# Four attention layers over eight images on one core: a fourth place for the exponentials, and a later plan for the side work

## The reference, cut to what is computed

```python
x = layer0(x)   # group norm, qkv, 8 heads of 32 channels, projection, + x
x = layer1(x)   # below
x = layer2(x)   # group norm, qkv, 8 heads of 32 channels, projection, + the normed x
x = layer3(x)   # group norm, qkv, ONE head of 256 channels, projection, + x

def layer1(h):
    x = group_norm(h) + pos_emb
    s = sigmoid(conv1x1(silu(conv3x3(silu(conv1x1(x))))))      # spatial weights
    sh = group_norm(x)
    standard = attention(sh @ wq, sh @ wk, sh @ wv)            # 8 heads of 32
    multi = [attention((x * s) @ wq_i, sh @ wk_i, sh @ wv_i) for i in (0, 1)]   # 2 heads of 128
    fused = silu(concat(standard, multi) @ ff_w1 + b1) @ ff_w2 + b2
    return group_norm(fused @ out_w + out_b) + h
```

## Time and profile before

| what | us |
|---|---|
| median of 3 runs | 5251.7 |
| lowest and highest run | 5237.88, 5256.1 |
| the profiled execution, its own time | 5264.05 |
| span of its trace, first to last instruction | 5262.3 |
| PE busy in the span | 4914.8 |
| mean granted clock of PE, as a share of full | 0.948 |

### The profile page before, as it was taken

One profiled execution on the slowest core, in us unless ns is written; L12 is line 12 of the kernel. 1 busy time (PEld: TensorE's weight loads), 2 busy tenths in 40 slices (PEclk: granted clock), 3 DMA queues, 4 the chain that ended last, 5 costly groups with the idle time before them and its releaser, 6 DMA issues. The chain is left out here.

```text
span 5262.3 us, 62946 instructions
## 1 busy us (share of the span) xinstructions
PE 4914.8 (93%) x22016; PEld 2254.5 (43%) x22016; DVE 3047.0 (58%) x5432; ACT 2418.6 (46%) x4321; POOL 2868.2 (55%) x1649
## 2 busy tenths in 40 slices
PE   7789999999999999999999999999999999999888
PEld 3325334553335533354334633346333463345424
DVE  6455666366773666636665467555666456763462
ACT  3352555435553455524555245552555425553251
POOL 3472567436664466634667357563666535764362
PEclk8899989999999998999999999899989999999988
DMA  3111212021210211102210112201122012110110
GB/s 88 27 35 46 55 37 55 16 60 45 51 37 21 75 42 40 37 26 64 55 43 20 41 49 57 49 13 47 49 51 55 7 53 57 46 46 11 30 36 12
DMA packets 103606, 221.18 MB, mean 42 GB/s; under 512 B 31104, under 2 KB 33408, under 8 KB 103168
## 3 DMA queue, kind: packets, MB, share of 16 engines
q1 hardware_dynamic: 103296, 217.16, 16.0%
HBM read 56.47 MB, written 8.39 MB: 12 GB/s over the span
## 5 line engine op out<-in xcount | busy, mean ns | idle before, releaser
L855 ACT ACTIVATE probs<-bank 128x512 f32<-128x512 f32 x3456 | 1934.5, 599 | 2401.5 <-PE bank L517 2279.4
L958 DVE TENSOR_REDUCE max_cols<-bank 128x1 f32<-128x512 f32 x3456 | 2191.5, 681 | 1367.4 <-PE bank L517 1360.0
L1200 POOL TENSOR_TENSOR probs_added<-probs_added,probs 128x1024 f32<-128x1024 f32 x768 | 1796.8, 2373 | 83.5 <-ACT probs L855 83.4
L517 PE MATMUL bank<-q_stack,k_stack 97*128 97x512 f32 (+1 forms) x3584 | 1674.2, 523 | 63.8 <-DVE max_cols L958 32.1
L517 PE MATMUL bank<-probs,v_tokens 128*32 128x512 f32 (+1 forms) x7168 | 1373.7, 639 | 31.5 <-ACT probs L855 29.9
L1200 POOL TENSOR_TENSOR probs_added<-probs 128x1024 f32<-128x1024 f32 x192 | 454.0, 2370 | 1042.0 <-ACT probs L855 1040.3
L517 PEld LDWEIGHTS bank<-q_stack,k_stack 97*128 97x128 f32 (+1 forms) x3584 | 665.2, 195 | 799.7 <-issue 442.6
L517 PE MATMUL bank<-act,weight_stream 128*128 128x512 f32 x1792 | 937.1, 625 | 38.6 <-ACT act L865 27.4
L1187 POOL TENSOR_TENSOR probs_added<-probs_added,probs 128x512 f32<-128x512 f32 x288 | 368.4, 1279 | 623.5 <-ACT probs L855 622.2
L517 PE MATMUL bank<-high_parts 32*128 32x512 f32 x3072 | 403.7, 513 | 120.1 <-DVE max_cols L958 82.0
L517 PEld LDWEIGHTS bank<-probs,v_tokens 128*32 128x32 f32 (+1 forms) x7168 | 317.0, 122 | 444.4 <-issue 306.2
(11 more groups left out here) (84 smaller groups left out, 2929.9 us busy)
## 6 DMA issues: line engine op xcount, KB each, us to landing
k_stack<-high_parts SPq DMA_DIRECT2D x384, 128.0 KB, 2.4
q_stack<-high_parts SPq DMA_DIRECT2D x768, 64.0 KB, 2.0
weight_stream<-stream_dram SPq DMA_DIRECT2D x32, 768.0 KB, 4.3
k_stack<-low_parts SPq DMA_DIRECT2D x192, 128.0 KB, 2.4
q_stack<-low_parts SPq DMA_DIRECT2D x384, 64.0 KB, 2.0
act<-x_dram SPq DMA_DIRECT2D x8, 1024.0 KB, 6.5
act<-pos_dram SPq DMA_DIRECT2D x8, 1024.0 KB, 5.8
weight_stream<-stream_dram SPq DMA_DIRECT2D x16, 512.0 KB, 3.9
```

The source lines that it names most:

```text
L517: return nc.tensor.matmul(dst, lhsT, rhs, start=start, stop=stop, **kw)
L855: act.activation(PR[:, m % P_RING, j, :], bank[:, :], ACT.Exp, scale=att.scale).then_inc(reading(key), 1)
L958: dve.tensor_reduce(cols[:, kh, j, qt:qt + 1], bank[:, :], AX.X, ALU.max).then_inc(reading(key), 1)
L1200: pool.tensor_tensor(ADD[:, js, :], one, two, ALU.add).then_inc(p_added, 1)
```

## The change

PR gets a fourth place. Its memory is that of WLO, so SBUF use stays as it was. Narrow attentions use all four places, wide ones the first three; `places_of_probs` picks for each item the place that was used longest ago, and notes the item that was there before (`PRIOR`), for which ACT waits. DVE gets one wait, before it writes the first low part of k of "m": until PE and POOL are done with the last item in the fourth place. In the plan of between-work "1" the convolutions spread out, the second norm comes later, and q, k, v start 3 units later; in that of "2", q, k, v start 1.8 units later and the first quads 1 unit earlier. No instruction is added or removed on any engine but for these waits, and none changes its size.

```diff
-P_RING = 3
+P_RING = 4
...
-            each("stats", [("a",) + q for q in QUARTERS], 42, 1) + unit("sa1", 0, 2, 44) + unit("sa1", 1, 2, 46.5) + \
-            norm("norm", 47.2, 2.5, "a", "o") + unit("sa2", 0, 3, 54.5) + unit("sa2", 1, 3, 57.5) + \
-            tile("sa3", 0, 1, 63.6) + tile("sa3", 1, 1, 66.1) + [(65.9, "sa3 one", 0), (68.4, "sa3 one", 1)] + \
-            each("spatial", QUARTERS, 68.8, 1)
-        out = [(at + (4.8 if name == "apply" and i[0] == "norm" else 0), name, i) for at, name, i in out]
-        out += projections(group(0), 71.1, 1) + stacks(80, 2.3) + values(82.1, 2) + projections(group(1), 109.1, 1.7) + \
+            each("stats", [("a",) + q for q in QUARTERS], 41.5, 1.5) + unit("sa1", 0, 2, 43.5) + unit("sa1", 1, 2, 47.5) + \
+            norm("norm", 50.2, 2.5, "a", "o") + unit("sa2", 0, 3, 56) + unit("sa2", 1, 3, 59.5) + \
+            tile("sa3", 0, 1, 65.6) + tile("sa3", 1, 1, 69.1) + [(67.9, "sa3 one", 0), (71.4, "sa3 one", 1)] + \
+            each("spatial", QUARTERS, 71.8, 1)
+        out = [(at + (3.2 if name == "apply" and i[0] == "norm" else 0), name, i) for at, name, i in out]
+        out += projections(group(0), 74.1, 1) + stacks(82.5, 2.1) + values(84.1, 2) + projections(group(1), 109.1, 1.7) + \
             narrow_start(87, 120.5, 118, 4)
...
-            projections(group(0), 76.8, 1) + stacks(85.5, 2) + values(87, 2) + projections(group(1), 110.1, 1.6) + \
-            narrow_start(88, 121.5, 118, 4)
+            projections(group(0), 78.6, 1) + stacks(87, 1.8) + values(88.6, 1.9) + projections(group(1), 110.1, 1.6) + \
+            narrow_start(87, 121.5, 118, 4)
...
+def places_of_probs():
+    place, prior, last = [], [], [None] * P_RING
+    for m, (att, _) in enumerate(ITEMS):
+        p = min(range(P_RING - att.wide), key=lambda p: -1 if last[p] is None else last[p])
+        place.append(p)
+        prior.append(last[p])
+        last[p] = m
+    return place, prior
...
-        WLO = sb("wide_low", [P, CT, T], F32R)
...
+        WLO = sb("wide_low", [P, CT, T], F32R, at=pr_at + (P_RING - 1) * 4 * HALF * 4)
...
-                if j == 0 and m >= P_RING:
-                    act.wait_ge(p_used, m - P_RING + 1)
-                    added = added_before(*ITEMS[m - P_RING])
+                if j == 0 and PRIOR[m] is not None:
+                    act.wait_ge(p_used, PRIOR[m] + 1)
+                    added = added_before(*ITEMS[PRIOR[m]])
...
+                    if att.kind == "m" and name == "k" and i == (0, 0):
+                        m = max(m for m in range(att.item0) if PLACE[m] == P_RING - 1)
+                        dve.wait_ge(p_used, m + 1)
+                        dve.wait_ge(p_added, added_before(*ITEMS[m]))
```

More of the change, by code:

```diff
@@ L252 @@
 ITEMS = [(a, i) for a in ATTS for i in range(a.units // 4)]
+def places_of_probs():
[6 more added lines that the diff above has]
+    return place, prior
+PLACE, PRIOR = places_of_probs()
 def plan():
@@ L576, in narrow_probs @@
             def narrow_probs(att, s, i):
-                return PR[:, (att.item0 + 8 * s + i) % P_RING, :, :]
+                return PR[:, PLACE[att.item0 + 8 * s + i], :, :]
             def values_narrow(att, s, i):
@@ L606, in values_wide @@
                 keys = [("av", att.index, s), ("av2", att.index, s)][:att.ctiles]
-                probs = PR[:, (att.item0 + 2 * s + kt // 4) % P_RING, kt % 4, :]
+                probs = PR[:, PLACE[att.item0 + 2 * s + kt // 4], kt % 4, :]
                 for d, key in enumerate(keys):
@@ L854, in score @@
                 bank = until_full(act, key)
-                act.activation(PR[:, m % P_RING, j, :], bank[:, :], ACT.Exp, scale=att.scale).then_inc(reading(key), 1)
+                act.activation(PR[:, PLACE[m], j, :], bank[:, :], ACT.Exp, scale=att.scale).then_inc(reading(key), 1)
             for event, it, i in PLAN:
@@ L1180, in score @@
                     until_read(pool, key)
-                    one, two = (PR[:, (att.item0 + v // 4) % P_RING, v % 4, :] for v in (u - 1, u))
+                    one, two = (PR[:, PLACE[att.item0 + v // 4], v % 4, :] for v in (u - 1, u))
                     if r == 1:
@@ L1193, in score @@
                     m, js = att.item0 + u // 4, slice(j - 1, j + 1)
-                    one, two = PR[:, (m - 1) % P_RING, js, :], PR[:, m % P_RING, js, :]
+                    one, two = PR[:, PLACE[m - 1], js, :], PR[:, PLACE[m], js, :]
                     if i == 1 and j == 1:
```

## The result

The changed kernel takes 5192.2 us (median of 4 runs, 5188.1 to 5196.6) beside 5244.8 for the kernel before on the same chip: a ratio of 0.9892, 95% interval 0.9867 to 0.9916, or 52.6 us less. The forecast was 5150. The time lies outside the forecast's own range (5120 to 5185) and inside the range for 8 in 10 (5092 to 5218), 42 us from the forecast and 10 from the rival "the clock falls as before" (5202).

A forecast was written before the change was run, and what follows sets the result against it. PE's idle time (347.5 us) and half clock (274 us) were taken as the bound. Savings of 56 + 29 + 23 = 108 us gave 5156, and half of 12.35 more gave 5150; own range 5120 to 5185, 8 in 10 5092 to 5218.

The forecast's parts named there:

- the clock falls as before: Rival, chance 0.25: idle time goes (55 us), but half clock lasts as long as before; some 5202 us.
- The sum: Whole kernel: 56 (between-work "1"), 29 (between-work "2") and 23 us (fourth place) make 108 us saved.
- What bounds the kernel: Whole kernel: PE's idle time, 347.5 us, and half clock, 274 us; attention "1" beside "3" at full clock.
- Idle time at unit 50: Between-work "1", units 49 to 53: PE's waits fall from 3.43 to 1.2 us, saving 15 us over seven stretches.
- The clock behind it: After unit 50's waits, attention "2" beside "1": four of seven clock falls go, 41 of 71.6 us.
- The argument from attention "1": Attention "1" beside "3": similar idle time, spread over a stretch, goes with clock 1.00; used to support the 41 us.
- q, k, v of between-work "2": Attention "0" beside "2": the 3.00 us before k's first product falls to 0.6, 17 us, plus 12 of clock: 29.
- The fall at unit 40 ... I keep: Attention "0" beside "2": the half-clock stretch at unit 40, 13.7 us in the row shown, stays.
- The fourth place, alone on the engines: Three attentions running alone: some 7.8 us less each, 23 us in all; waits move from ACT to PE.
- In the loaded stretches ... I count 0: Attentions beside between-work: the fourth place gives 0, as POOL is far from busy there.
- The jam at unit 66: Rival, chance 0.08, units 64 to 68: a new PE stop and clock fall cost 19 us a sample; 5342 at full price.
- What would show it.: Signs: attention "2" about 156.5 us at clock 0.95 or more in most, "0" near 159, attentions alone about 8 less each.

The follow-up runs named there:

- group 2: Runs on one chip: kernel before (mean 5255.0 us), the changed kernel again (5206.5), and three variants of the changed kernel (5203.9, 5205.9, 5159.0).
- the repeat: The changed kernel measured again without further edits, six runs beside the kernel before: mean 5206.5 us, ratio 0.9906 (0.9887 to 0.9926).
- the later statistics: Changed kernel with the residual's statistics 2 units later, norm and q, k, v 1 unit later in between-work "2": 5205.9 us, 0.9905 of before.
- the lighter steps: In attentions running alone POOL makes eight adds, not ten; PE multiplies the item by ones: 0.9811 of before on the changed kernel, 1.0037 on the kernel before.
- split mixes: Changed kernel with the three DVE instructions of each sa1 mix in three successive units: mean 5203.9 us, 0.9902 of before.
- group 3: Runs on one chip: kernel before (25 runs, mean 5239.7 us) and four kernels with edits to POOL's adds (5163.9, 5223.9, 5189.4, 5258.7).

## Why the prediction was right, and where it was wrong

- **The sum.** The 108 us were 55 of idle time and 53 of clock (41 and 12). In the means of group 2 the change takes 49 us: 38 at full clock and 11 of clock. Both terms were too large, the second most. That 5150 came within 42 us owes something to luck: the first four runs lost only 225 us to half clock, six later ones 242.
- **What bounds the kernel.** Right in the main: idle time of PE and its clock. "3" beside "m" stayed as it was. Attention "1" beside "3", untouched by the edit, didn't: one of seven stretches had 6.8 us of half clock, and in the repeat's profile three of seven, up to 13.6 us.
- **Idle time at unit 50.** 3.43 us went to 1.96 (1.22 + 0.49 + 0.25), where I put 1.2. The quad's wait was to fall to 0.3 and rose from 1.02 to 1.22: at unit 47 the mix comes right behind the last statistics of the convolution's input, which I left out of DVE's account, and "mean" now waits for its own "aggr". "var" lost its 1.68 as foreseen.
- **The clock behind it.** This is the step that failed: "I take four of seven falls as gone", 41 us. None went. 143.1 us at half clock became 112.8 at that place, and another 34.0 appeared near unit 67 behind 0.35 us of waits; on the other side, the 6.8 us near unit 105, in five of seven samples before, are in none after. Beside the place the plan of "1" gives 10 us in time where I forecast 56 in all. The rival "the clock falls as before" had it right at unit 50.
- **The argument from attention "1".** It was to show that idle time spread over a stretch goes with full clock. In the repeat's profile one such stretch takes 137.1 us at 0.95:

```profile
842.90:980.00 137.10, 133.05 (x679) 56.20 (x680) 80.66 (x143) 78.47 (x146) 95.14 (x45) 0.95 0.13 34
```

```profile
869.11 0.51 PE L532 MATMUL bank<-high_parts 32*128 32x512 f32 x4 [0.39 <-DVE max_cols L973]
```

  The clock falls at 871.8, for 13.6 us. PE's waits in the 39 us before are 0.32, 0.75, 0.39 and 0.39. In all seven stretches of the kernel before they are the same within 0.01 us, at the same places, and the clock doesn't fall. Nor does it in four of the repeat's own seven, with these waits again. So the waits alone don't decide whether it falls; what does, no run here shows. The Trainium skill ("TensorE: Matmul & The Clock Gate", "A second HAM failure mode: psum-queue depth-cycling") tells of a kernel whose clock went up and down behind small idle times between groups of products. The traces agree at unit 50, where 2.0 us in three pieces went with seven falls of seven, and less at unit 76 (next point).
- **q, k, v of between-work "2".** 29 us forecast, 28 by the timed kernels beside the place, 37 by the two profiles. The half-clock stretches at unit 76, in all seven samples before, are in none after and in two (3.4 us each) in the repeat's profile: here "the clock falls as before" was wrong and my 12 us about right. The 3.00 us became 1.35 in three pieces, where I said 0.6: ACT, which still has its four applies among the exponentials, now lets PE wait for banks.

```profile
1238.38 1.06 PE L532 MATMUL bank<-probs,v_tokens 128*32 128x512 f32 x8 [0.46 <-ACT probs L870]
1239.80 0.51 PE L532 MATMUL bank<-high_parts 32*128 32x512 f32 x4 [0.35 <-ACT probs L870]
1240.85 1.10 PE L532 MATMUL bank<-act,weight_stream 128*128 128x512 f32 x2 [0.54 <-ACT probs L870]
```

- **"The fall at unit 40 ... I keep".** In the profile after it went in five of seven samples and a new one came at unit 51. In the repeat's profile it is back in six of seven, so the change didn't take it away for good. ACT reaches the first norm's first apply before POOL has its coefficients, and PE waits behind it for 1.44, 0.46 and 0.46 us. In the profile before, where units 40 to 50 ran at half clock, POOL had these coefficients in time; that the low clock hid the lateness is my reading of the two traces, and no run tests it.

```profile
1205.99 0.81 ACT L880 ACTIVATE act<-act,gn_shift,gn_scale 128x512 f32<-128x512 f32 x1 [1.23 <-POOL gn_shift L1238]
```

```profile
1207.34 0.73 PE L532 MATMUL bank<-q_stack,k_stack 97*128 97x512 f32 x2 [1.44 <-ACT probs L870]
1208.53 0.73 PE L532 MATMUL bank<-q_stack,k_stack 97*128 97x512 f32 x2 [0.46 <-ACT probs L870]
1209.71 1.08 PE L532 MATMUL bank<-probs,v_tokens 128*32 128x512 f32 x4 [0.46 <-ACT probs L870]
```

- **The fourth place, alone on the engines.** Right in mechanism and close in size over the stretches: 23 us forecast, 19.6 in the profiles. (A step's ten adds come to 23.4 us, not 23.7; nothing hangs on it.) PE's own rows show the same 19.6 as 8.2 us less idle time and 11.4 less busy time, at a clock of 0.94 instead of 0.90; the forecast had reckoned without the clock. POOL's rest between steps went from 5.75 to 3.81 (forecast 3.6), and from 3.33 to 3.24; PE waits for POOL at the product named, and ACT for POOL only once, 2.1 us. The product begins 0.05 us after the last add (169.59 + 18.63 = 188.22).

```profile
109.75 2.36 POOL L1220 TENSOR_TENSOR probs_added<-probs 128x1024 f32<-128x1024 f32 x1 [3.81 <-ACT probs L870]
...
164.90 4.73 POOL L1220 TENSOR_TENSOR probs_added<-probs 128x1024 f32<-128x1024 f32 x2 [3.24 <-ACT probs L870]
169.59 18.63 POOL L1220 TENSOR_TENSOR probs_added<-probs_added,probs 128x1024 f32<-128x1024 f32 x8
```

```profile
105.99 1.06 PE L532 MATMUL bank<-probs_added,ones 128*32 128x512 f32 x8 [1.73 <-POOL probs_added L1220]
...
188.27 1.46 PE L532 MATMUL bank<-probs_added,ones 128*32 128x512 f32 x8 [2.61 <-POOL probs_added L1220]
```

- **"In the loaded stretches ... I count 0".** Not right in the total: alone, the place lost in clock elsewhere what it gained. Its 1.0009 (0.9991 to 1.0026) leaves no room for 20 us.
- **The jam at unit 66** did not come: the waits there are 0.35 us.
- **"What would show it."** By its own signs the forecast is half right. Attention "0" came to 158 us a stretch (159 named) and the attentions alone to 6.5 less each (8 named). Attention "2" came to 160.2 (156.5 named) at clocks of 0.89 to 0.94, where "0.95 or more in most" was to be seen, and half-clock stretches did turn up in other places, at unit 51 in attention "0" and at unit 67 in attention "2".
- **Still open:** what makes the clock fall or not behind the same waits; why the three kernels with the place and at most one plan lose 256 to 261 us to half clock, beside 247 before; how much of the full change's gain is clock, 11 us in the one comparison that gives both clocks, about as much as means over a few runs differ by.

## What to carry to other kernels

Price idle time of PE at what it is, and the clock's fall behind it as a gain only when a run shows it. In the loaded stretches the new plan of the convolutions cut 3.43 us of waits to 1.96 and the later statistics cut 2.53 to 1.33, and the clock still fell near both places. Eight adds instead of ten, which took PE's waits for POOL out of whole stretches, went with 37 us less lost to half clock. When a wait is taken from one engine, name the chain that is the next bound; here it was POOL's, and moving work off it was worth nearly as much as the whole change. And test two parts together before one is called worthless: alone, the fourth place left the kernel's time where it was and the lighter steps made it longer; together, beside the new plans, they gave the fastest kernel of this series. An engine's long wait costs nothing by itself: ACT's 3.70 us delayed no product, its 1.85 us did.

## What the runs showed of the hardware that was not expected

- PE at 1.2 GHz with nothing to wait for does not always come back to 2.4 at once: with split mixes one stretch lasted 34.1 us with PE busy 33.99 of it, and in another sample with the same instructions 13.7 us.
- The clock can fall behind waits behind which it elsewhere stays. In attention "1" beside "3" four waits of 0.32 to 0.76 us, the same within 0.01 us each time, went with full clock in all seven samples before, and in the repeat with full clock in four samples and with half clock for 3.4 to 13.6 us in three.
- Single executions of the kernel before spread from 5199.9 to 5264.4 us in group 3, with a correlation between time and granted clock near -0.9. Four runs of each kernel left an interval 0.5% wide (0.9867 to 0.9916).
